# One core, four layers: the first attention stage and the first feed-forward stage interleaved tile by tile, with expert weights streamed per tile

## The reference

```
x = x + attn_a(layernorm(x))   # gated linear attention: 32 heads of 4, 2 decays; a scan over time
x = x + ffn(layernorm(x))      # 8 experts, all used: acc += (silu(x @ Wg[e]) * (x @ Wu[e])) @ Wd[e]
x = x + attn_b(layernorm(x))   # softmax attention, causal, 16 heads of 8, one key/value head
x = x + ffn(layernorm(x))      # the same 8 experts again
```

## Time and profile before

| | |
|---|---|
| median of 3 runs | 1953.6 us (1953.53 to 1953.88) |
| the profiled execution, its own time | 1950.02 us |
| its span, first to last instruction | 1948.2 us |
| PE busy in the span | 1700.6 us, 87% |
| DVE, ACT, POOL busy | 1412.5 (73%), 1026.3 (53%), 572.8 us (29%) |
| granted PE clock, mean | 0.928 of full |
| moved by DMA | 20.14 MB, 10 GB/s over the span |

### The profile page before, as it was taken

One profiled execution on the slowest core, in us unless ns is written; L12 is line 12 of the kernel. 1 busy time (PEld: TensorE's weight loads), 2 busy tenths in 40 slices (PEclk: granted clock), 3 DMA queues, 4 the chain that ended last, 5 costly groups with the idle time before them and its releaser, 6 DMA issues.

```text
span 1948.2 us, 26315 instructions
## 1 busy us (share of the span) xinstructions
PE 1700.6 (87%) x7480; PEld 1301.4 (67%) x7480; DVE 1412.5 (73%) x2367; ACT 1026.3 (53%) x1765; POOL 572.8 (29%) x441
## 2 busy tenths in 40 slices
PE   3677676599999999999688898999699999999998
PEld 2344344387787778787366666666487787778787
DVE  6899998667777777777367666665577777777776
ACT  1121111166666666655376766767566666666665
POOL 1455555501101110400167666767501101110100
PEclk8788777599999999999699989989899999999999
DMA  2000001100000000100000000000100000000001
GB/s 77 0 1 0 0 0 33 50 1 16 16 1 16 16 0 0 33 1 1 0 1 1 1 1 0 0 1 1 33 1 17 17 0 17 16 0 0 0 1 43
DMA packets 23716, 20.14 MB, mean 10 GB/s; under 512 B 1626, under 2 KB 19166, under 8 KB 23646
## 3 DMA queue, kind: packets, MB, share of 16 engines
q1 hardware_dynamic: 23646, 19.29, 3.3%
HBM read 17.18 MB, written 2.10 MB: 10 GB/s over the span
## 4 chain that ended last, share of the span: by engine, by line
PE 69%; DVE 10%; issue 9%; POOL 7%; ACT 3%; DMA 0%; SPq 0%; DVEq 0%; POOLq 0%; ACTq 0%
PE pair L347 12%; PE pair L349 12%; PE pair L348 12%; PE bank L347 7%; PE bank L348 6%; PE bank L349 6%; POOL ARENA_R L735 3%; DVE XN L390 2%; DVE ARENA_R L1348 2%; PE pair L1168 2%; POOL ARENA L646 1%; DVE ARENA L457 1%; PE pair L1097 1%; PE pair L1098 1%; DVE ARENA L1486 1%
## 5 line engine op out<-in xcount | busy, mean ns | idle before, releaser
L1344 DVE TENSOR_TENSOR ARENA<-ARENA,pair 128x512 f32<-128x512 f32 x512 | 351.5, 687 | 289.9 <-PE pair L349 212.8
L772 ACT ACTIVATE ARENA<-bank 128x512 f32<-128x512 f32 x512 | 304.2, 596 | 347.2 <-PE bank L349 345.8
L347 PE MATMUL pair<-ARENA_R 128*128 128x512 f32 (+1 forms) x1080 | 427.2, 396 | 32.4 <-DVE ARENA_R L1348 17.9
L348 PE MATMUL pair<-ARENA_R 128*128 128x512 f32 (+1 forms) x1080 | 421.9, 391 | 0.0
L349 PE MATMUL pair<-ARENA_R 128*128 128x512 f32 (+1 forms) x1080 | 421.9, 391 | 0.0
L1348 DVE TENSOR_TENSOR ARENA_R<-ARENA,ARENA_R 128x512 fp32r<-128x512 f32 x512 | 375.6, 735 | 11.9
L766 ACT ACTIVATE ARENA_R<-ARENA 128x512 fp32r<-128x512 f32 x512 | 321.2, 627 | 64.5 <-DVE ARENA L1344 64.0
L735 POOL TENSOR_TENSOR ARENA_R<-ARENA,ARENA_R 128x512 fp32r<-128x512 f32 x192 | 250.3, 1317 | 120.2 <-ACT ARENA L909 115.5
L347 PEld LDWEIGHTS pair<-ARENA_R 128*128 128x128 f32 x1080 | 203.8, 189 | 86.3 <-DVE ARENA_R L1348 23.0
L589 POOL CAST ARENA_R<-ARENA 128x1536 fp32r<-128x1536 f32 x12 | 23.2, 1937 | 756.4 <-PE pair L349 756.4
L349 PEld LDWEIGHTS pair<-ARENA_R 128*128 128x128 f32 x1080 | 203.6, 189 | 42.8
(11 more groups left out here) (207 smaller groups left out, 2463.8 us busy)
## 6 DMA issues: line engine op xcount, KB each, us to landing
ARENA<-in_L_ffn_Wg_dram SPq DMA_DIRECT2D x16, 256.0 KB, 2.7
ARENA<-in_L_ffn_Wu_dram SPq DMA_DIRECT2D x16, 256.0 KB, 3.1
ARENA<-in_L_ffn_Wd_dram SPq DMA_DIRECT2D x16, 256.0 KB, 3.6
X<-in_L_attn_a_x_dram SPq DMA_DIRECT2D x8, 256.0 KB, 6.5
out_dram<-X SPq DMA_DIRECT2D x8, 256.0 KB, 2.3
CST<-in_tables_dram SPq DMA_DIRECT2D x1, 832.5 KB, 4.7
ARENA<-in_tables_dram SPq DMA_DIRECT2D x1, 768.0 KB, 4.3
CST<-in_tables_dram SPq DMA_DIRECT2D x1, 259.0 KB, 4.9
```

Of the source, the lines that this page charges most:

```text
L347: pe.matmul(dst, wh, xh, start=start, stop=False)
L348: pe.matmul(dst, wh, xl, start=False, stop=False)
L772: act.activation(SG[:, k % 2, :], bank[k % 2], ACT.Silu).then_inc(s.sil, 1)
L1344: v.tensor_tensor(HF[:, k, :], SG[:, k % 2, :], bank[2 + k % 2], ALU.mult).then_inc(s.mul, 1)
```

## The change

Attention A and F1 become one stage. A step t has 32 slots c (`CH`, one for each chunk of 8 experts x 4). In slot c every engine first does chunk c of the feed-forward of tile t-2 and then a small piece of attention for tile t (or t-1, t+1), by a table of `if c == ...` in `attn`. Steps run from -1 to 9: steps 0 and 1 have attention alone, steps 2 to 7 both, steps 8 and 9 the feed-forward of tiles 6 and 7 with the last pieces of tile 7. F2 has the same form without attention.

With tiles outside and experts inside, each tile needs all experts' weights again: they are loaded, rounded (`hi_part`, ACT) and subtracted (`lo_part`, POOL) 64 times a stage instead of 8, in parts of 512, one expert ahead. The down products of a tile's 32 chunks stay in one PSUM bank, so `YACC`, its clearing and the adds go; ACT copies the sum out once a tile (`take_down`). The down product is three chunks behind instead of two. Every fourth lo subtraction of the hidden part moves from DVE to POOL (`hidden_lo` in `ffn_pool`). The three normalisations of attention A and F1 move from DVE to ACT (Identity with scale and bias). Attention A's step is no longer pipelined against the step before, except for its output projection and what follows it. The norms of F2's input leave attention B, but for tile 0, and are done one tile ahead inside F2. All loops of the feed-forward stages are written out. In attention B the stages' order is as before, and the normed input and `Q2` have one buffer each instead of two.

```diff
-        YACC = take(NT, TOK)
...
+        def load_part(sp, x, part):
+
+            after(sp, F.wl, 3 * (x - 2) + part + 1)
+            dst = WS[:, x % 2, part, :]
+            src = (f_Wg, f_Wu, f_Wd)[part][x % NE]
+            if part == 2:
+                dst, src = dst.rearrange("p (k c) -> p k c", k=FC), src.rearrange("(k p) c -> p k c", p=P)
+            sp.dma_start(dst, src).then_inc((F.wload0, F.wload1)[x % 2], 16)
+
+        def hi_part(act, x, part):
+
+            act.wait_ge((F.wload0, F.wload1)[x % 2], 48 * (x // 2 + 1))
+            after(act, (F.gate, F.up, F.d)[part], FC * (x - 1))
+            act.activation(WH[:, x % 2, part, :], WS[:, x % 2, part, :], ACT.Copy).then_inc(F.wh, 1)
+
+        def lo_part(g, x, part):
+
+            g.wait_ge(F.wh, 3 * x + part + 1)
+            g.tensor_tensor(WL[:, x % 2, part, :], WS[:, x % 2, part, :], WH[:, x % 2, part, :].bitcast(F32),
+                            ALU.subtract).then_inc(F.wl, 1)
...
+        def part_at(f, c):
+
+            x = NE * f + c // FC + 1
+            part = {0: 0, 1: 1, 3: 2}.get(c % FC)
+            return None if part is None or x == NE * NT or x == 2 * NE * NT else (x, part)
...
+        def ffn_pe(pe, f, c):
+
+            G, x, k = CH * f + c, NE * f + c // FC, c % FC
+            u, cols = x % 2, slice(k * P, (k + 1) * P)
+            if c == 0:
+                pe.wait_ge(n_f.lo, f + 1)
+            if k == 0:
+                pe.wait_ge(F.wl, 3 * x + 1)
+            after(pe, F.sil, G - 1)
+            split_product(pe, bank[c % 2], WH[:, u, 0, cols], WL[:, u, 0, cols], XTH[:, f % 2, :],
+                          XTL[:, f % 2, :]).then_inc(F.gate, 1)
+            if k == 0:
+                pe.wait_ge(F.wl, 3 * x + 2)
+            after(pe, F.mul, G - 1)
+            split_product(pe, bank[2 + c % 2], WH[:, u, 1, cols], WL[:, u, 1, cols], XTH[:, f % 2, :],
+                          XTL[:, f % 2, :]).then_inc(F.up, 1)
+            if G - 3 >= base(G):
+                down(pe, G - 3)
+
+        def down(pe, G):
+
+            c, x, k = G % CH, G // FC, G % FC
+            u, cols = x % 2, slice(k * P, (k + 1) * P)
+            if c == 0:
+                after(pe, F.ys, G // CH)
+            if k == 0:
+                pe.wait_ge(F.wl, 3 * x + 3)
+            pe.wait_ge(*lo_done(G))
+            split_product(pe, bank[4], WH[:, u, 2, cols], WL[:, u, 2, cols], HH[:, k, :], HL[:, k, :],
+                          start=(c == 0), stop=(c == CH - 1)).then_inc(F.d, 1)
...
+        def ffn_act(act, f, c):
+
+            G = CH * f + c
+            act.wait_ge(F.gate, G + 1)
+            after(act, F.mul, G - 1)
+            act.activation(SG[:, c % 2, :], bank[c % 2], ACT.Silu).then_inc(F.sil, 1)
+            if G - 1 >= base(G):
+                hidden_hi(act, G - 1)
+            if part_at(f, c):
+                hi_part(act, *part_at(f, c))
+
+        def hidden_hi(act, G):
+
+            act.wait_ge(F.mul, G + 1)
+            after(act, F.d, G - 3)
+            act.activation(HH[:, G % FC, :], HF[:, G % FC, :], ACT.Copy).then_inc(F.hh, 1)
+
+        def hidden_lo(eng, G):
+
+            eng.wait_ge(F.hh, G + 1)
+            after(eng, F.d, G - 3)
+            eng.tensor_tensor(HL[:, G % FC, :], HF[:, G % FC, :], HH[:, G % FC, :].bitcast(F32),
+                              ALU.subtract).then_inc(lo_done(G)[0], 1)
...
+        def take_down(act, f):
+
+            act.wait_ge(F.d, CH * (f + 1))
+            after(act, F.back, f)
+            act.activation(YS[:, :], bank[4], ACT.Copy).then_inc(F.ys, 1)
+
+        def ffn_pool(g, f, c):
+
+            G = CH * f + c
+            if c % FC == 0 and G - 1 >= base(G):
+                hidden_lo(g, G - 1)
+            if part_at(f, c):
+                lo_part(g, *part_at(f, c))
+
+        def ffn_dve(v, f, c):
+
+            G = CH * f + c
+            v.wait_ge(F.up, G + 1)
+            v.wait_ge(F.sil, G + 1)
+            if G >= FC:
+                v.wait_ge(*lo_done(G - FC))
+            v.tensor_tensor(HF[:, c % FC, :], SG[:, c % 2, :], bank[2 + c % 2], ALU.mult).then_inc(F.mul, 1)
+            if G - 1 >= base(G) and (G - 1) % FC != FC - 1:
+                hidden_lo(v, G - 1)
...
+            def scan(t, m, c):
+                v.wait_ge(A.beta, t + 1)
+                if c < 4:
+                    v.wait_ge(a_used[f"v{c}"], t + 1)
+                    after(v, (A.num0, A.num1)[m], t)
+                else:
+                    v.wait_ge(A.phi_k, t + 1)
+                    after(v, A.den, t)
+                v.tensor_tensor_scan(S[:, m, c, :], BETA[:, m, :], KV[:, c, :], 0.0, ALU.mult,
+                                     ALU.add).then_inc(A.scan, 1)
+
+            def product(t, comps, n):
+                v.wait_ge(A.scan, 10 * t + n)
+                v.wait_ge(A.phi_q, t + 1)
+                a, b = comps
+                v.tensor_tensor(S[:, 0, a:b, :], S[:, 0, a:b, :], spread(PQ[:, :], b - a),
+                                ALU.mult).then_inc(A.prod0, 1)
...
+                    if c == 10:
+                        phi(t, 1)
+                        key_value(t, 0)
+                    if c == 11:
+                        scan(t, 0, 4)
+                        key_value(t, 1)
+                    if c == 12:
+                        scan(t, 0, 0)
+                        key_value(t, 2)
+                    if c == 13:
+                        scan(t, 0, 1)
+                        key_value(t, 3)
+                    if c == 14:
+                        scan(t, 0, 2)
+                    if c == 15:
+                        scan(t, 0, 3)
+                    if c == 16:
+                        scan(t, 1, 4)
+                        product(t, (4, 5), 1)
+                    if c == 17:
+                        scan(t, 1, 0)
+                        product(t, (0, 2), 3)
+                    if c == 18:
+                        scan(t, 1, 1)
+                        product(t, (2, 4), 5)
+                    if c == 19:
+                        scan(t, 1, 2)
+                    if c == 20:
+                        scan(t, 1, 3)
...
-            run_steps(pe, step)
-            ffn_pe(pe, 0)
+            for t in range(-1, NT + 2):
+                for c in range(CH):
+                    f = t - 2
+                    if is_tile(f):
+                        ffn_pe(pe, f, c)
+                    attn(t, c)
+            for G in range(NT * CH - 3, NT * CH):
...
-            for s in f:
-                if s is f[1]:
-                    sp.wait_ge(f[0].wl, NE)
-                    load_expert(sp, s, 0, 0)
-                    load_expert(sp, s, 1, 1)
-                with sp.Fori(1, NE // 2) as h:
-                    load_expert(sp, s, 2 * h, 0)
-                    load_expert(sp, s, 2 * h + 1, 1)
```

1446 lines of the change are left out of this document (712 added, 734 removed).

## The result

The changed kernel takes 1871.33 us (median of 4, 1870.55 to 1873.11) against 1953.57 (median of 4, 1953.49 to 1953.88): ratio 0.958, interval 0.9563 to 0.9597. The profiled execution took 1873.11 us at a span of 1871.3, so 1.8 us lie around the span as before, and the spans differ by 76.9 us.

The account below looks back on a forecast made before the run. DVE bounds attention A and PE bounds F1 and F2; interleaved, the DVE-POOL lock limits slots 9 to 22. Joint stage -53, attention B -10, B to F2 -13.5, F2 -7: -83.5 from 1953.6 gives 1870 us, range 1818 to 1926.

Parts of the forecast that it names:

- six steps with both: Joint stage, attention A and F1 together: PE 88 us + 13 lost + 2 of low clock = 103 each, between 94 and 112.
- step 8: Joint stage, plain feed-forward chunks with tile 7's last attention work: 65.3 + 1.7 + 1.1 = 68 us.
- tail, product 31 to the end of the copy: Joint stage's last chunk: product 0.69, hi 0.63, POOL's lo 1.28, down 0.68, copy 0.6: 3.9 us.
- attention B: PE's stalls behind the early norm, some 4 us a tile in three or four tiles, go: -10 us, between 0 and -20.
- F2, first gate to the copied sum: Second feed-forward stage: 522.4 + 14 turns of 0.45 + 3.3 at the end + about 1 at low clock = 533 us, -7.
- PE's own need: PE's work in a step with attention A and F1: chunks 65.3 and attention 22.2, together 88 us.
- The clock's term: In steps with attention A and F1, PE's clock falls in stalls: at most 2 us a step on top.
- ACT's slot 8: Two table loads and four activations delay silu 9: the dense stretch begins 7.5 us behind gate 8's end instead of about 3.
- Rival 1: Steps with attention A and F1: the lock hardly matters, the stretch hides; step 93 us, 1810 us in all; chance 0.17.
- Rival 2: Steps with attention A and F1: POOL becomes the limit; step 112 us, +54, 1924 us in all; chance 0.22.
- Rival 3: Steps with attention A and F1: the lock alternates, each locked DVE instruction waiting a POOL one; 124 us, 1996 in all; chance 0.08.
- Rival 4: Written-out feed-forward loops: PE's straight-line instruction fetch costs time; if half hidden 110 us, 1980 in all; chance 0.03.

Follow-up runs that it names:

- e1: Changed kernel with POOL's weight lo subtractions 4 columns wide instead of 512 in the joint stage, from the third expert on (computation partly left out): 1826.8 us.
- e7: Changed kernel with attention A's scans on 8 columns instead of 512 from the second tile on (computation partly left out): 1818.5 us.
- e3: Changed kernel with attention A's two exponentials replaced by Identity, so a step's two ACT table loads go (elu not computed): 1873.9 us.
- e4: Changed kernel with POOL's every fourth hidden lo subtraction given back to DVE in both feed-forward stages: 1852.2 us.
- e9: Changed kernel with slots moved: F2's next-tile norm and tile 7's two norms later, POOL's preparation of attention B earlier: 1855.7 us.
- e8: Changed kernel loading only the first two experts' weights, once, and using them for all later experts (computation partly changed): 1871.4 us.
- e6: Changed kernel with weight parts' lo subtractions moved from POOL to DVE, one slot later, except each stage's first expert: 1850.9 us.
- e12: Changed kernel with e9's slots, e4's edit, clearing at slot 12, preparation at 28 to 30, F1's input norm two slots later, mix tanh before exponentials: 1857.3 us.

## Why the prediction was right, point by point

| step of the prediction | forecast | measured |
|---|---|---|
| steps 0 and 1, first projection to first gate | 96 | 91.3, and the first product 2.4 later than usual |
| six steps with both | 6 x 103 | 6 x 100.3 |
| step 8 | 68 | 76.1 |
| step 9, first gate to product 31 | 66 | 65.3 |
| tail, product 31 to the end of the copy | 3.9 | 11.3 |
| end of the joint stage | 873 (-53) | 869.7 (-56.3) |
| attention B | -10 | 429.1 to 422.0 (-7.1), and 2.0 less ahead of it |
| B to F2 | -13.5 | 13.9 to 0.2 (-13.7) |
| F2, first gate to the copied sum | 533 (-7) | 542.8 (+3.4), and 1.2 less behind it |
| sum over the span | -83.5 | -76.9 |

The range held, and the mechanism is the one forecast. That the median came out 1.3 us from the forecast is luck: the span fell by 6.6 us less than forecast, with the six steps 16 us too long in the sum and step 8, the tail and F2 too short by 8, 7 and 10, and 5.4 us of the difference were hidden because the profiled execution of after lies 1.8 us above its median where that of before lay 3.6 below.

**The step with both.** The mechanism was right in the main: the loss stands in slots 9 to 22, where DVE and POOL hold each other up. PE's own need was put at 88 us and is 87.65 (e1). Over it stand 9 us of waits and 3.6 us of low clock (91.3 busy against 87.65), where 13 and 2 were forecast. e1 and e7 show that half or more of what is over is caused in slots 9 to 22, by POOL's subtractions as by DVE's scans: either taken away gives 6 to 8 of the 12.6 us, of which 3.6 and 3.2 are PE's time at the lower clock. The clock's term was put at 2 at most. But the terms inside were mis-sized. The scans (1.354), phi (1.10) and lo (0.735) that the sum took from the earlier trace rows held waits for POOL already: alone they take 1.21, 0.66 and 0.68. So DVE's work without waiting was put too high and its waits, about 11 us a step (5.3 in lo, 3.6 in scans, some 2 in products, each mean less the shortest), were put too low. And ACT's slot 8, 4.5 us in the forecast's 58.5, was no term of its own: POOL's residual add is as late (e3).

**Rivals.** Rival 1 (step 93) fails: with POOL's weight lo cut to 4 columns the step is 6 us shorter (e1), so they do cost. Rival 2 (POOL the limit, 112) was too strong, but its mechanism is there: 1.5 us of PE's waits are for a weight lo, DVE waits for POOL's residual add, and taking 8 of its 43 instructions of 512 columns from POOL gave 2.7 us (e4). Rival 3 (124) fails: a step is 100.3. Rival 4, the fetch of straight-line code, shows nowhere: the 31 chunks of step 9 take 63.73 us with PE busy 63.73, 2.04 us for most of them, as in the loops of before. The Trainium skill held this fetch to be mostly hidden (Runtime: NRT & Kernel Launch, section on instruction fetch mechanics); the trace agrees.

**Step 8 and the tail** are one place where a term of the forecast failed: "65.3 + 1.7 + 1.1" took tile 7's remaining work as a sum of PE's instructions. It is a chain through DVE, POOL and ACT laid out for slots of 3 us, and in chunks of 2 us each engine stands in front of it (e9 takes out 4 to 6 of the 8 us). The tail left out what POOL has ahead of its last hidden lo; with that lo on DVE it is 3.7 us (e4), the 3.9 of the sum.

**F2** is the largest term put too low, and its sign was wrong: -7 forecast, +3.4 measured. The 66.5 us a tile became 67.5, which is 8 of the 9.8 us. The loads are hidden as said (e8), but ACT's wait in slot 12 for POOL's small norm group, which stands behind weight parts, was not in the sum. With the norm two slots later a tile is 66.3 (e9), and with the weight lo on DVE, where the wait is gone, it is 66.3 too (e6).

**Attention B** gave 7.1, not 10, and the two traces show why. Before, PE waited five times about 2.2 us for what stood behind the early norm, whose four normalisations took 3.49 us of DVE at one of these places (first line below: sum, times and longest; a sixth wait is short); after, this wait is gone in every tile. But the norm of F2's first tile, now done at B's end, makes a new one: ACT stands 3.8 us for POOL's small norm group, and PE 6.3 us for ACT:

```profile
PE bank L347 <- DVE ARENA L1617: 11.1, 6, 2.2
...
1291.63 1.65 ACT L421 ACTIVATE ARENA<-X,SM 128x128 f32<-128x128 f32 x4 [3.81 <-POOL SM L401]
1294.77 1.22 PE L1272 MATMUL pair<-ARENA_R 128*128 128x512 f32 x2 [6.27 <-ACT ARENA L1002]
```

The forecast had the first and not the second. No run takes the second away.

## What to carry to other kernels

When two stages are interleaved, add up per engine, and then add the two engines that exclude each other as one: here, by an estimate from the shortest instructions, POOL's 55 us of work with two SBUF inputs and DVE's 35 fill 90 of a step's 100. The sum is a warning and not the step's time: e6 takes it from 90 to 76, and the step falls by 1.0. Take the durations for such a sum from the shortest instructions of a kind, since a mean holds waits already. Such work belongs on the engine that is faster at it, up to the slots where that engine is full.

A table of slots fits one speed. Where a step runs faster than the chain in it was laid out for (the first and last steps, the stage without attention), look for the engine that stands in front of something not ready, and for what is queued behind: step 8, the tail and F2's slot 12 cost some 24 us over the forecast together, and moving them by guess moved some of the stalls. The small norm group on POOL with ACT, and then PE, behind it is such a place three times over, in F2, at the end of attention B and in e12.

## What was not expected of the hardware

A POOL copy with one SBUF input (0.61 us for 512 columns) excludes DVE's two-input instructions as a subtraction does: 0.94 us instead of 0.68 for DVE, 1.00 instead of 0.61 for the copy. A POOL subtraction 4 columns wide still took 0.43 us in the mean (e1, 24 a step; the shortest 0.20), so narrow ones are not free.
